# Cross-attention with two passes over the keys: scoring the second pass's first three units before the maxima are known

## The reference

```python
x = x + xattn(layernorm(x), ctx, ctx, mask)      # softmax(q k^T / sqrt(16)) v over 12544 keys
x = x + attn(layernorm(x), Wqvk, Wo)             # causal self-attention, 128 rows
x = x + ffn(layernorm(x), w_gate, w_up, w_down)  # with fake quantization
```

## Time and profile before

| what | value |
|---|---|
| median of 3 runs | 473.27 us (471.38 to 475.01) |
| profiled execution | 471.32 us, of which its span 469.6 us |
| mean granted clock of PE | 0.992 |
| first pass to the last rough score of PE | 0 to 221.0 us |
| seam: end of the maxima's fold | 227.86 us |
| second pass: first score to last exp | 229.26 to 421.2 us |

### The profile page before, as it was taken

One profiled execution on the slowest core, in us unless ns is written; L12 is line 12 of the kernel. 1 busy time (PEld: TensorE's weight loads), 2 busy tenths in 40 slices (PEclk: granted clock), 3 DMA queues, 4 the chain that ended last, 5 costly groups with the idle time before them and its releaser, 6 DMA issues.

```text
span 469.6 us, 16264 instructions
## 1 busy us (share of the span) xinstructions
PE 444.4 (95%) x6464; PEld 351.2 (75%) x6464; DVE 349.1 (74%) x483; ACT 387.5 (83%) x492; POOL 99.9 (21%) x101
## 2 busy tenths in 40 slices
PE   7998999999999999996899999999999999999896
PEld 4766667766677676772598999999999999986463
DVE  5789999999999999999559988445555344605566
ACT  7788888888888888876598999999999999992433
POOL 1698532333323333316000000000000000000000
PEclk9999999999999999997999999999999999999999
DMA  8997556755567655966998898788789788100000
GB/s 264 350 382 257 208 216 260 298 221 215 208 250 298 242 207 214 365 244 229 411 359 275 289 302 298 263 295 291 262 313 331 263 294 274 72 5 0 1 2 13
DMA packets 33258, 111.99 MB, mean 238 GB/s; under 512 B 4048, under 2 KB 10576, under 8 KB 33232
## 3 DMA queue, kind: packets, MB, share of 16 engines
q1 hardware_dynamic: 29056, 105.07, 60.7%
q0 software_dynamic: 4032, 6.42, 4.7%
q10 hardware_dynamic: 144, 0.13, 0.1%
HBM read 74.44 MB, written 33.96 MB: 231 GB/s over the span
## 4 chain that ended last, share of the span: by engine, by line
PE 68%; DVE 14%; issue 7%; ACT 6%; DMA 4%; SPq 0%; POOL 0%; DVEq 0%; ACTq 0%; POOLq 0%
PE ps_a L1113 21%; PE ps_k L1127 20%; PE ps_a L968 9%; PE ps_k L959 9%; DVE block_max L717 4%; PE ps_a L1002 4%; ACT early L514 4%; DVE early L722 3%; DMA k_lo_scratch<-k_lo 3%; DVE k_lo L683 1%; DVE early L753 1%; DMA early<-in_ctx 1%; PE ps_a L1294 1%; ACT k_stack L467 1%; PE ps_k L1311 1%
## 5 line engine op out<-in xcount | busy, mean ns | idle before, releaser
L717 DVE TENSOR_REDUCE block_max<-ps_a 128x2 f32<-128x896 f32 x112 | 121.0, 1083 | 0.0
L1113 PEld LDWEIGHTS ps_a<-q_stack,k_stack 64*128 64x128 f32 x1568 | 94.4, 187 | 12.6 <-issue 12.1
L1113 PE MATMUL ps_a<-q_stack,k_stack 64*128 64x128 f32 x1568 | 102.4, 277 | 0.4 <-DVE q_stack L763 0.4
L514 ACT CAST early<-ps_a 128x896 bf16<-128x896 f32 x104 | 94.6, 910 | 6.1 <-PE ps_a L1002 6.1
L585 ACT ACTIVATE middle<-ps_a 128x1024 f32<-128x1024 f32 (+1 forms) x84 | 92.0, 1168 | 4.7 <-PE ps_a L1113 1.7
L585 ACT ACTIVATE early<-ps_a 128x1024 f32<-128x1024 f32 (+1 forms) x84 | 92.0, 1170 | 3.3
L968 PE MATMUL ps_a<-w_hi,k_stack 128*128 128x256 f32 x392 | 68.5, 297 | 0.0
L722 DVE TENSOR_TENSOR early<-early 128x896 bf16<-128x896 bf16 x104 | 66.2, 636 | 0.5
L959 PE MATMUL ps_k<-k_stack,w_hi 128*128 128x448 f32 x224 | 60.8, 391 | 4.1 <-issue 1.3
L968 PEld LDWEIGHTS ps_a<-w_hi,k_stack 128*128 128x128 f32 x392 | 53.0, 188 | 11.3 <-issue 11.2
L1002 PE MATMUL ps_a<-k_hi,q_pair 32*128 32x448 bf16 x448 | 42.7, 370 | 10.0 <-ACT early L514 8.6
(11 more groups left out here) (198 smaller groups left out, 495.4 us busy)
## 6 DMA issues: line engine op xcount, KB each, us to landing
k_stack<-k_hi_scratch SPq DMA_DIRECT2D x68, 448.0 KB, 5.3
v_scratch<-early SPq DMA_DIRECT2D x14, 952.0 KB, 5.2
v_in<-v_scratch SPq DMA_DIRECT2D x14, 952.0 KB, 6.0
k_hi_scratch<-k_hi SPq DMA_DIRECT2D x28, 448.0 KB, 2.5
k_lo_scratch<-k_lo SPq DMA_DIRECT2D x16, 448.0 KB, 3.3
k_stack<-k_lo_scratch SPq DMA_DIRECT2D x16, 448.0 KB, 5.6
ctx_b<-in_ctx SPq DMA_DIRECT2D x7, 896.0 KB, 6.8
early<-in_ctx SPq DMA_DIRECT2D x6, 896.0 KB, 6.9
```

Of the source, the lines that this page charges most:

```text
L514: nc.scalar.copy(staged[:, u % 2], pair_scores(u, 0)).then_inc(max_copied, 1)
L717: nc.vector.tensor_reduce(block_max[:, 2 * u:2 * u + 2, par], pair_scores(u, 1), AX.X, ALU.max).then_inc(max_taken, 1)
L1113: last = nc.tensor.matmul(ps_a[:, base + bank, at * Q:(at + 1) * Q], k_stack[half, b_par, a, t * P:(t + 1) * P], q_stack[half, a, ab, :], ...
```

## The change

PE now scores the units 0 to 2 during the fold, with the maxima rows of `q_stack` still zero. It runs 5 fillers, then these scores (they wait for ACT's last copy and DVE's last reductions, since they use the same banks, and for the keys), then 15 fillers. When the maxima are there, a new function `lower` adds the negated maximum to each finished score in PSUM: one matmul per 128 x 128 cell, with a column of `neg_max`, broadcast to 128 columns, as weights and `eye_b` as the moving tensor. Only `lower` raises `scored` for these three units. The rows of maxima, which all later units need in `q_stack`, are made after the first unit's lowering, four groups of four matmuls, and they go to the partitions 32, 96, 0 and 64 of `attended`, that is of `ps_k`. DVE copies all four groups (1 x 512 each) to `q_stack`; ACT copies none. `attended` is zeroed only after the copies, by a matmul that waits for `rows_set`. The five fillers in front of the loop are gone. `prob_slots_free` is raised by 6 after the early scores.

```diff
-MAX_ROWS = (32, 96)
+MAX_ROWS = ((32, 96), (0, 64))
...
-WARM_FOLD = 23
-WARM_PASS = 5
+WARM_FOLD = (5, 15)
...
         def max_rows(ab, part):
-            row, a = MAX_ROWS[ab], part * PR // 2
+            row, a = MAX_ROWS[part][ab], part * PR // 2
             return (q_stack[row:row + 1, a:a + PR // 2, ab, :],
-                    ps_a[row:row + 1, 3 + 2 * part:5 + 2 * part, :].rearrange("p n (a b q) -> p (n a) b q", a=2, b=2)[:, :, ab, :])
+                    attended[row:row + 1, :].rearrange("p (a q) -> p a q", a=PR // 2))
...
-            act.wait_ge(q_spread, 8)
-            for part in range(2):
-                act.wait_ge(max_rows_ready, 2 * part + 2)
-                nc.scalar.mul(*max_rows(0, part), 1.0).then_inc(first_rows_set, 1)
...
             dve.wait_ge(q_spread, 8)
             for part in range(2):
-                dve.wait_ge(max_rows_ready, 2 * part + 2)
-                nc.vector.tensor_scalar(*max_rows(1, part), 1.0, None, ALU.mult).then_inc(second_rows_set, 1)
+                for ab in range(2):
+                    dve.wait_ge(max_rows_ready, 2 * part + ab + 1)
+                    nc.vector.tensor_scalar(*max_rows(ab, part), 1.0, None, ALU.mult).then_inc(rows_set, 1)
...
                 pe.wait_ge(hi_ready, NB * DC * 2)
-                keep_clock(attended, WARM_FOLD)
-
-                pe.wait_ge(row_max_ready, NB + 1)
-                pe.wait_ge(v_evacuated, NB * NV)
-                columns = [head for u in range(NG) for _, head in group_heads(u)[1]]
-                for h in range(H):
-                    last = nc.tensor.matmul(ps_a[MAX_ROWS[h % 2]:MAX_ROWS[h % 2] + 1, 3 + h // 4, (h % 4) * Q:(h % 4 + 1) * Q], neg_max[:, columns.index(h):columns.index(h) + 1], eye_b[:],
-                                            start=True, stop=True)
-                    if h % 4 == 3:
-                        last.then_inc(max_rows_ready, 1)
-
-                nc.tensor.matmul(attended, zeros_b[:, 0:P], zeros_b[:], start=True, stop=True,
-                                 skip_group_check=True).then_inc(prob_slots_free, SLOTS_P)
-                pe.wait_ge(q_spread, 8)
-                pe.wait_ge(consts_set, 8)
+                keep_clock(attended, WARM_FOLD[0])
...
+                def lower(u):
+                    for k, (t, a) in enumerate(GROUPS[u]):
+                        for ab in range(2):
+                            bank, at = cell(u, k, ab)
+                            head = columns.index(2 * a + ab)
+                            last = nc.tensor.matmul(ps_a[:, UNIT_BANK[u] + bank, at * Q:(at + 1) * Q],
+                                                    neg_max[:, head:head + 1].to_broadcast([P, P]), eye_b[:], start=False,
+                                                    stop=True, skip_group_check=True)
+                    last.then_inc(scored, 1)
+
+                def row_of_maxima(ab, part):
+                    row = MAX_ROWS[part][ab]
+                    for n in range(PR // 2):
+                        head = columns.index(2 * (part * PR // 2 + n) + ab)
+                        last = nc.tensor.matmul(attended[row:row + 1, n * Q:(n + 1) * Q], neg_max[:, head:head + 1], eye_b[:],
+                                                start=True, stop=True)
+                    last.then_inc(max_rows_ready, 1)
+
+                pe.wait_ge(q_spread, 8)
+                pe.wait_ge(consts_set, 8)
                 arrive(0, 0, 0)
+                pe.wait_ge(max_copied, (NB - 1) * NG)
+                pe.wait_ge(v_evacuated, NB * NV)
                 for u in range(NU):
-                    if u != 1:
-                        pe.wait_ge(first_rows_set, u // 2 + 1)
-                        pe.wait_ge(second_rows_set, u // 2 + 1)
-                    score(0, u, 1)
-                for _ in range(WARM_PASS):
-                    nc.tensor.matmul(attended, zeros_b[:, 0:P], zeros_b[:], start=False, stop=False, skip_group_check=True)
+                    pe.wait_ge(max_taken, NB * NG - 1 + u // 2)
+                    last = score(0, u, 1)
+                last.then_inc(prob_slots_free, SLOTS_P)
+                keep_clock(attended, WARM_FOLD[1])
+
+                pe.wait_ge(row_max_ready, NB + 1)
+                lower(0)
+                for part in range(2):
+                    for ab in range(2):
+                        row_of_maxima(ab, part)
+                lower(1)
+                lower(2)
+                pe.wait_ge(rows_set, 4)
+                nc.tensor.matmul(attended, zeros_b[:, 0:P], zeros_b[:], start=True, stop=True, skip_group_check=True)
                 with pe.Fori(0, NB // 2 - 1) as i:
```

More of the change, by code:

```diff
@@ L188, in perceiver_layer @@
         row_max_ready, max_rows_ready = sem("row_max_ready"), sem("max_rows_ready")
-        first_rows_set, second_rows_set = sem("first_rows_set"), sem("second_rows_set")
+        rows_set = sem("rows_set")
         scored, exp_done, prob_slots_free = (sem(n) for n in ("scored", "exp_done", "prob_slots_free"))
@@ L1117, in score @@
                                 last.then_inc(shared_scored, 1)
-                    last.then_inc(scored, 1)
+                    return last
                 def add_up(b_par, u, slot):
@@ L1157, in two_blocks @@
                                     arrive(i * 2 + 1, 1, 1)
-                                score(nxt // UNITS, nxt % UNITS, i * (2 * UNITS // NU) + w // NU + 2)
+                                score(nxt // UNITS, nxt % UNITS, i * (2 * UNITS // NU) + w // NU + 2).then_inc(scored, 1)
                         if u % UNITS == 0:
@@ L1164, in two_blocks @@
                             add_up(w // UNITS, w % UNITS, w % SLOTS_P)
+                columns = [head for u in range(NG) for _, head in group_heads(u)[1]]
+                def lower(u):
[7 more added lines that the diff above has]
+                    last.then_inc(scored, 1)
```

## The result

The changed kernel takes 478.62 us (median of 8 runs, 476.38 to 479.56), the kernel before 472.20 us (median of 8, 471.38 to 475.01): slower by a ratio of 1.0115, 95% interval 1.0086 to 1.0144. The ratio takes in all executions, so it differs a little from the quotient of the medians (1.0136): the loss is 6.4 us by the medians and 5.4 us by the ratio, where a gain of 0.5 us was forecast, and the time is outside of the stated range. The profiled execution took 479.56 us, its span is 477.9 us, 8.3 more than before.

What follows compares the result with a forecast made beforehand. PE was taken to set the second pass's pace, so an earlier loop start is kept: 0.26 + 0.23 = 0.49 us gained, 471.32 to 470.8 us profiled, 473.27 to 472.8 on the runs' scale; range 470.4 to 475.1.

Steps and rivals of the forecast that it cites:

- What bounds the kernel: Second pass: PE sets the pace at 3.41 us a round, so an earlier start of the steady rounds is kept.
- The clock ahead of the maxima: Seam: clock rises at 223.2 after five fillers; early scores run at full clock to 224.78, fillers behind them to 228.02.
- (a): Rival, 20%: the clock ahead of the maxima rises later; fillers end at 228.84, 0.82 us later; result 0.3 us slower.
- The clock behind the copies: Seam: PE waits some 1.4 us for the four copies; the forecast itself counts no loss of clock there.
- (b): Rival, 15%: the clock falls while PE waits for the copies; 1.0 us slower, up to 3.4 us lost.
- The 81 ns: Skill's time per weight load and matmul, a 0.4 us loss here; the forecast took 0.056 us from the trace instead.
- More than (b) at its worst: What being slower by over 1% was said to need; it was given 3%.
- lowering and first exp: Seam: the first unit's lowering takes 0.45 us, to 228.47; its exp starts at about 228.65 in place of 229.96.
- the copies: Seam: DVE's four copies of maxima rows take 2.55 us, to 231.43, and become the longest thing there.
- S2: Time of the loop's first scores behind the seam: 232.17 before, 4.31 us after the maxima; forecast 231.91.
- The 0.26 us gained at S2: End of the seam: the loop's first scores come at 231.91 in place of 232.17.
- The 0.23 us of round 1: Loop's first round: PE no longer waits for the third unit's exp, so 3.41 us in place of 3.64.

Runs made afterwards that it cites:

- fill12: Changed kernel with 12 fillers ahead of the early scores and 5 behind, in place of 5 and 15: 474.09 us, ratio 1.0056 to the kernel before.
- fill18: Changed kernel with 18 fillers ahead of the early scores and none behind: 474.45 us, ratio 1.0066 to the kernel before.
- fill0: Changed kernel with no filler ahead of the early scores and 20 behind: 479.39 us, one run.
- before4dve: Kernel before with all four copies of maxima rows on DVE, none on ACT: 476.25 us, ratio 1.0085 to the kernel before.
- b4gap: before4dve with 6 fillers in the gap where PE waits for the first two copies: 473.24 us, ratio 1.0029 to the kernel before.
- rowsfirst: fill12gap with the rows of maxima made before the first unit's lowering and 6 fillers in the gap: 474.10 us, ratio 1.0045 to the kernel before.
- pad: Kernel before with its 23 fillers split into 16 and 27 shorter ones, 20 more matmuls in the same time: 474.10 us, ratio 1.0044.
- fill12gap: fill12 with 8 fillers in the gap where PE waits for the copies: 474.27 us, ratio 1.0047 to the kernel before.
- looped: rowsfirst with all fillers of the seam in three loops of PE, one matmul per body: 474.26 us, ratio 1.0041 to the kernel before.
- split: Changed kernel with the copies of maxima rows shared by ACT and DVE again: 479.39 us, ratio 1.0178 to the kernel before.
- gapfill: Changed kernel (5 and 15 fillers) with 8 more fillers while PE waits for the copies: 476.59 us, ratio 1.0093 to the kernel before.

## Why the prediction was wrong

**What bounds the kernel** was right: every microsecond by which PE's rounds were late came to the end (pieces of 8.1 us, span 8.3).

**The clock ahead of the maxima** is the first step that failed: "PE runs five fillers first, at half clock as before ... The clock is then up". The forecast took over the time of the rise from the old trace, though the change replaces what PE does at just this time. In the changed kernel the rise came at 229.0 and not at 223.2; fill12, fill18 and fill0 show that it follows the fillers and not the scores. The low stretch lasted 10.2 us in place of 6.8. Even with 6.8 us the rise would have come at 225.6, since this execution's fall was 2.4 us later, which the one trace of before could not show. Rival (a) had the late rise, but with 20% and with a rise at 3.73 us: 0.8 us lost, where 2.8 were (the lowering at 230.78, forecast 228.02). It counted scores as being as good as fillers.

**The clock behind the copies** is the second: the forecast saw 1.4 us of idle time and gave rival (b) 15%. With the same copies, fill12 and fill18 have 1.75 us (in the changed kernel the record of the zeroing is missing, and the 2.06 us shown take it in). Before4dve and b4gap show that gaps of 1.1 us and 0.2 us can be enough. Its price was mis-sized even more: "half of the time until the clock is back, 2.2 to 3.7 us", and 6.8 us at worst. The low stretch behind the copies lasted 3.4 us in fill18, 6.8 in fill0 and 10.2 in before4dve and the changed kernel, where rounds 2 and 3 lost 4.7 us with PE busy throughout. The price had been taken from a place where fillers brought the clock up. Why it took so long in some executions and not in others is open. "More than (b) at its worst" for slower by over 1% was wrong since (a) and (b) could come together, and did.

**The page cited for (b)**: the Trainium skill, page "TensorE: Matmul & The Clock Gate", section "HAM oscillation — how this bites in real kernels", was cited for (b). The traces now agree that a wait between bursts of matmuls can make the next burst slow, though the waits of the page's kernel last some 3 to 5 us and the ones here 1.1 to 1.75 us. The 81 ns of the same page's section "Back-to-back issue gap" did not hold here: in rowsfirst 28 lowerings took 1.74 us, which is 0.056 us each ((1.74 - 0.22) / 27).

**The plain terms** held to 0.4 us, but the gain was smaller than that: lowering and first exp 0.65 us (0.63), the copies 2.84 us (2.55 forecast; steps of 0.72 in place of 0.62, why is not known), from the lowering's start to S2 4.25 us in fill12 (3.89). The 0.26 us gained at S2 are eaten by that: in fill18, with the clock up and the lowering in time, S2 comes 4.32 us behind the maxima, beside 4.31 before. The 0.23 us of round 1 are gained (3.41 us from S2 to the next round in fill12). The seam of rowsfirst gains 0.66 us, but in an order that the forecast was not about.

**The code's length** was in no term and no rival. Pad costs about 2 us, four times the forecast gain, which is as much as both repairs left: fill12gap is at a ratio of 1.0047, pad at 1.0044. Looped, which was to win it back, did not, so how the cost goes with the length stays open.

No version here is faster than the kernel before; the changed seam with all repairs is level with pad.

## What to carry to other kernels

A duration at a given clock belongs to what the engine does around it: before moving real matmuls into the place of fillers, ask which of them keep the clock, and price a fall by how long the work behind it takes to bring the clock back, from a trace where that very work runs. A wait of a microsecond on such an engine can cost four, as before4dve shows. When a change adds instructions to an engine that sets the pace, test the same number of harmless ones on the old kernel: if that alone costs as much, the idea isn't what failed.

## What was not expected of the hardware

- PE busy without a gap did not mean a rising clock: 10.2 us of scores and add-ups ran at 0.50 in the changed kernel. In fill18 the same work ran at 0.50 for 3.4 us.
- With the same gap of 1.75 us, one profiled execution kept its clock (fill12) and another lost it for 3.4 us (fill18), so such kernels scatter: fill12 from 472.34 to 478.57 us.
- 20 more matmuls of unchanged total time in unrolled code cost 0.44% (0.13 to 0.75), with stalls of 0.6 to 1.3 us at fixed places in a loop several rounds later.
- Stalls inside the loop were joined by a low clock of their own in split (1.36 us), gapfill (1.43) and fill18 (0.97), for 3.4 to 6.8 us; with stalls of 1.25 to 1.32 us in pad, fill12gap and looped the clock stayed up.
